# dt of every fourth unit of a selective scan: spread by DMA from rows in DRAM instead of by TensorE

## The reference

```
x = x + layer(layernorm(x))            # layer: below
x = x + ffn(layernorm(x))              # silu(x W1) * (x W3), Hadamard, W2
# layer: h = u + mamba(rmsnorm(u));  h + (silu(g) * up) @ down.T   (704 wide)
# mamba: z, x, B, C, dt_raw = split(rmsnorm(u) @ in_proj.T)
dt = softplus(dt_raw @ dt_proj.T + bias)          # 256 channels
for t in range(1024):                              # per channel, 32 states
    h = exp(dt[t] * A) * h + dt[t] * x[t] * B[t]
    y[t] = sum over states of h * C[t]
```

## Time and profile before

| | before |
|---|---|
| median of 3 runs | 1200.27 us |
| profiled execution | 1197.15 us |
| its span, first to last instruction | 1195.4 us |
| PE / PEld busy | 1069.9 / 539.2 us |
| DVE busy | 1021.0 us |
| POOL busy | 925.3 us |
| ACT busy | 603.6 us |
| scans run from | 51.2 to about 1091 us |
| moved by DMA | 176.38 MB |

### The profile page before, as it was taken

One profiled execution on the slowest core, in us unless ns is written; L12 is line 12 of the kernel. 1 busy time (PEld: TensorE's weight loads), 2 busy tenths in 40 slices (PEclk: granted clock), 3 DMA queues, 4 the chain that ended last, 5 costly groups with the idle time before them and its releaser, 6 DMA issues.

```text
span 1195.4 us, 12998 instructions
## 1 busy us (share of the span) xinstructions
PE 1069.9 (90%) x3848; PEld 539.2 (45%) x3848; DVE 1021.0 (85%) x1161; ACT 603.6 (50%) x1092; POOL 925.3 (77%) x564
## 2 busy tenths in 40 slices
PE   2577679999999999999998999899998989997988
PEld 1222124545544464446444554546453554445535
DVE  3379889999999989999999999999999999995322
ACT  3645366555654455555754555646654554443120
POOL 0479999878998889887998899878998898774000
PEclk9676559999999999999999999999999999899989
DMA  5898877765767676776768676867667576540000
GB/s 216 192 251 190 191 170 159 163 154 128 193 154 164 136 174 156 171 162 142 182 140 177 139 180 138 185 137 173 168 144 163 122 178 151 130 89 18 1 1 18
DMA packets 99493, 176.38 MB, mean 148 GB/s; under 512 B 12960, under 2 KB 21600, under 8 KB 98784
## 3 DMA queue, kind: packets, MB, share of 16 engines
q1 hardware_dynamic: 98272, 171.36, 62.9%
q0 software_dynamic: 1152, 4.19, 1.0%
HBM read 150.34 MB, written 8.39 MB: 133 GB/s over the span
## 4 chain that ended last, share of the span: by engine, by line
PE 56%; POOL 13%; DVE 10%; issue 10%; ACT 5%; DMA 3%; SPq 1%; DVEq 0%; POOLq 0%; ACTq 0%
PE p_r L444 17%; PE p_r L433 13%; POOL h_s L939 8%; PE p_r L439 8%; PE p_dt L388 7%; PE p_y L399 6%; DVE h_s L752 5%; PE p_r L450 3%; POOL bt_s L919 3%; DVE bt_s L737 2%; DMA bt_s<-dx_rows 2%; ACT p_dt L526 2%; ACT tok L543 1%; PE p_r L423 1%; ACT tok L541 1%
## 5 line engine op out<-in xcount | busy, mean ns | idle before, releaser
L939 POOL TENSOR_TENSOR h_s<-h_s,c_s 128x1024 f32<-128x1024 f32 x256 | 604.2, 2361 | 86.8 <-DVE h_s L752 76.6
L526 ACT ACTIVATE p_dt<-p_dt,an_s 128x512 f32<-128x512 f32 x512 | 331.3, 658 | 327.5 <-PE p_dt L388 327.1
L388 PE MATMUL p_dt<-kdt,pick_s 128*128 128x512 f32 x512 | 327.8, 665 | 47.3 <-DVE h_s L752 46.9
L752 DVE TENSOR_TENSOR_SCAN h_s<-p_dt,carry,bt_s 128x512 f32<-128x512 f32 x256 | 321.2, 1272 | 8.2 <-ACT p_dt L526 5.8
L752 DVE TENSOR_TENSOR_SCAN h_s<-p_dt,bt_s 128x512 f32<-128x512 f32 x256 | 305.1, 1212 | 26.0 <-ACT p_dt L526 15.8
L444 PE MATMUL p_r<-nT,w_s 128*128 128x512 f32 x512 | 243.9, 605 | 3.2 <-ACT nT L677 3.1
L919 POOL TENSOR_TENSOR bt_s<-bt_s,b_s 128x1024 f32<-128x1024 f32 x96 | 227.1, 2366 | 13.8 <-DMA bt_s<-dx_rows 13.7
L737 DVE TENSOR_TENSOR bt_s<-bt_s,p_b 128x1024 f32<-128x1024 f32 x160 | 192.5, 1203 | 5.1 <-DMA bt_s<-dx_rows 5.1
L388 PEld LDWEIGHTS p_dt<-kdt,pick_s 128*128 128x128 f32 x512 | 100.4, 202 | 204.5 <-DVE h_s L752 128.7
L433 PE MATMUL p_r<-nT,gu_s 128*128 128x512 f32 x352 | 169.4, 605 | 2.7 <-ACT nT L672 2.7
L399 PE MATMUL p_y<-h_s,ysel_s 128*32 128x512 f32 x1024 | 148.0, 652 | 16.6 <-POOL h_s L939 16.6
(11 more groups left out here) (86 smaller groups left out, 734.5 us busy)
## 6 DMA issues: line engine op xcount, KB each, us to landing
bt_s<-dx_rows SPq DMA_DIRECT2D x512, 256.0 KB, 5.3
kdt<-st_dt SPq DMA_DIRECT2D x64, 128.0 KB, 5.3
tok<-in_x SPq DMA_DIRECT2D x8, 512.0 KB, 7.1
xr_s<-xb_s SPq DMA_DIRECT2D x64, 64.0 KB, 3.9
dx_rows<-dx_s SPq DMA_DIRECT2D x16, 256.0 KB, 5.1
b_s<-xb_s SPq DMA_DIRECT2D x64, 64.0 KB, 4.9
xo<-in_x SPq DMA_DIRECT2D x8, 512.0 KB, 7.1
out<-res POOLq DMA_DIRECT2D x8, 512.0 KB, 5.5
```

The source lines that it names most:

```text
L388: nc.tensor.matmul(p_dt[DT_BANK[u]][:, :], sel, kdt[:, h, p // 16, :], start=True, stop=True)\
L526: A(p_dt[DT_BANK[u]][:, :], p_dt[DT_BANK[u]][:, :], ACT.Exp, scale=an_s[:, c:c + 1]).then_inc(a_dA, 1)
L752: V.tensor_tensor_scan(h_s[:, u % 8, :], p_dt[DT_BANK[u]][:, :], bt_s[:, u % 16, :], carry[:, u:u + 1] if par else 0.0, ALU.mult, ALU.add) ...
L939: G.tensor_tensor(h_s[:, two, :], h_s[:, two, :], c_s[:, h, :].unsqueeze(1).broadcast_to([P, 2, T]), ALU.mult)\
```

## The change

From the second tile on (i >= 1), units 3, 7, 11, ..., 63 (`ROW_UNITS`, 16 of 64) get no `spread`. Instead `keep_rows` also writes `dt_s` to DRAM (`dt_rows`), and `load_row_pair` reads the rows of two such units, each row repeated over 32 partitions, into a new tile `dtr4_s` of four places. `decay` of such a unit reads `dtr4_s` and still writes the PSUM bank `p_dt`, once the scan that used the bank last is done. Nothing else is reordered.

```
+ROW_UNITS = range(3, U, 4)
+def by_row(i, u):
+    return i >= 1 and u in ROW_UNITS
+def spreads(i, u):
+    return u + 1 if i == 0 else U + (i - 1) * (U - len(ROW_UNITS)) + u + 1 - made(ROW_UNITS, u)
...
+            def load_row_pair(t, par, q):
+                sp.wait_ge(l_dt_rows, ((t - 1) * 2 + q // 4 + 1) * 16)
+                sp.wait_ge(a_dA, t * U + 8 * q - 8)
+                for g in range(GH):
+                    rows_of_g = dt_rows[par, q // 4].rearrange("(a b g) t -> g a b t", a=4, g=GH)[g, 3]
+                    src = rows_of_g[2 * (q % 4):2 * (q % 4) + 2]
+                    sp.dma_start(dtr4_s[NS * g:NS * g + NS, 2 * (q % 2):2 * (q % 2) + 2, :],
+                                 src.partition_broadcast(NS)).then_inc(l_row4[q % 2], 16)
             def keep_rows(t, par, h):
+                if t >= 1:
+                    sp.wait_ge(a_dt, t * 2 + h + 1)
+                    sp.dma_start(dt_rows[par, h], dt_s[:, :]).then_inc(l_dt_rows, 16)
...
                 for u in range(U):
+                    if u % 8 == 2:
+                        q = u // 8 + 1
+                        if (units and i >= 1 if q < 8 else units and pre):
+                            load_row_pair(i + q // 8, par if q < 8 else 1 - par, q % 8)
...
-                    if (units if u + 2 < U else pre):
+                    if not by_row(i + (u + 2) // U, (u + 2) % U) and (units if u + 2 < U else pre):
                         spread(i + (u + 2) // U, (u + 2) % U)
...
-                act.wait_ge(pe_dt, i * U + u + 1)
                 c = UH * (u // UH) + unit_channel(u)
-                A(p_dt[DT_BANK[u]][:, :], p_dt[DT_BANK[u]][:, :], ACT.Exp, scale=an_s[:, c:c + 1]).then_inc(a_dA, 1)
+                if by_row(i, u):
+                    q = u // 8
+                    act.wait_ge(l_row4[q % 2], ((i - 1) * 4 + q // 2 + 1) * 64)
+                    act.wait_ge(v_sc, i * U + u - DT_GAP[u] + 1)
+                    dt_in = dtr4_s[:, u // 4 % 4, :]
+                else:
+                    act.wait_ge(pe_dt, spreads(i, u))
+                    dt_in = p_dt[DT_BANK[u]][:, :]
+                A(p_dt[DT_BANK[u]][:, :], dt_in, ACT.Exp, scale=an_s[:, c:c + 1]).then_inc(a_dA, 1)
...
                         act.wait_ge(g_dx, m)
+                        if m > 2:
+                            act.wait_ge(l_dt_rows, (m - 2) * 16)
                     A(dt_s[:, :], v, ACT.Copy).then_inc(a_dt, 1)
```

More of the change, by code:

```diff
@@ L128, in build @@
         bt_s = sb("bt_s", [P, RUN * 4, T])
+        dtr4_s = sb("dtr4_s", [P, 4, T])
         h_s = sb("h_s", [P, 8, T])
@@ L163, in build @@
         l_x, l_xo, l_xrep, l_out = sem("l_x"), sem("l_xo"), sem("l_xrep"), sem("l_out")
-        l_rows = sem("l_rows")
+        l_rows, l_dt_rows = sem("l_rows"), sem("l_dt_rows")
+        l_row4 = [sem(f"l_row4{k}") for k in range(2)]
         l_dx = [sem(f"l_dx{k}") for k in range(4)]
@@ L193, in build @@
         dx_rows = nc.dram_tensor("dx_rows", [2, 2, P, T], F32).ap()
+        dt_rows = nc.dram_tensor("dt_rows", [2, 2, P, T], F32).ap()
         x_t = x.rearrange("b s d -> (b s) d")
@@ L268, in load_dt @@
             def load_dt(t, h):
-                made_dt, spread_dt = number(t * 2 + h + 1), number((t - 1) * U + UH * (h + 1))
+                made_dt, spread_dt = number(t * 2 + h + 1), spreads(t - 1, UH * (h + 1) - 1) if t else 0
                 sp.wait_ge(a_dth, made_dt)
```

## The result

The changed kernel takes 1191.97 us (median of 4 runs, 1191.76 to 1193.68) against 1200.3 us for the kernel before beside it (1199.26 to 1201.45): ratio 0.9934, 95% interval 0.9916 to 0.9951. It gained 8.3 us; 17.3 were forecast. The direction held, and so did the outer range (1169 to 1200 us); the forecast band of 1176 to 1190 us was missed by 2 us, and the size is less than half of the forecast.

A forecast was written before the change was run, and what follows sets the result against it. TensorE and VectorE were both nearly full in tiles 1 to 7, with TensorE leading the last chain. 1197.15 - 19.3 + 1.6 = 1179.5 us, 1182.6 as a median, stated as 1183; band 1176 to 1190, outer range 1169 to 1200 us.

The forecast's parts named there:

- A spread's price: On TensorE: each spread costs 0.23 us, so 112 removed spreads take 25.8 us off it.
- Part B: Gate/up/down phase: five spreads fall away, 1.15 us per tile, 8.0 us over 7 tiles; bounds 0 and 12.6 us.
- Part A: End of the tile: w2's last group no longer cut by unit 63's spread; 0.55 us in six tiles, 3.3 us.
- the seam's 1.15: End of the tile: the second half of w2's last group starts 1.15 us earlier once both halves are one piece.
- Part C: w1/w3 phase: five spreads go and the wait behind the second softplus comes earlier; 1.15 us per tile, 8.0 us.
- The sum: Whole kernel: 3.3 + 8.0 + 8.0 = 19.3 us gained from the removed spreads.
- rival 2: Tiles 1 to 7: VectorE is the bound and the rest is hidden; 0 to 2 us gained, 1199 us; chance 0.12.
- The clock: Gap behind the down projection: TensorE's clock fell in one tile of seven; one more fall forecast, costing 1.6 us.
- rival 1: Gaps behind the down projection: the clock falls in every one, six more falls cost 9.8 us; 1190.8 us; chance 0.14.
- The DMAs at nothing: Added row reads and writes: DMA share rises from 0.67 to 0.83 in tiles 1 to 7, costing no time.
- The five other units at nothing: Spreads of units 3, 7, 11, 35 and 59 lie where TensorE waits for others; removing them gains nothing.
- The markers: Signs to check in the profile, such as TensorE busy time down over 25 us, tile period about 129 us.

The follow-up runs named there:

- e5: Changed kernel with only unit 63 by row, against the kernel before: 1196.83 us, ratio 0.9971.
- e6: Changed kernel with only units 15, 19, 23, 27 and 31 by row, against the kernel before: 1196.86 us, ratio 0.9971.
- e7: Changed kernel with only units 39, 43, 47, 51 and 55 by row, against the kernel before: 1196.73 us, ratio 0.9979.
- e1: Changed kernel without the added DMAs, exps of the units by row reading a constant 0.01: 1193.25 us, ratio 0.9943 to the kernel before.
- e2: Kernel before with the added DMAs issued and waited for but unused, all spreads kept on TensorE: 1200.99 us, ratio 1.0005.
- e17: e9 with 11 units by row; 3, 7, 11, 35 and 59 are spread by TensorE again: 1186.8 us, ratio 0.9883 to the kernel before.
- e9: Changed kernel plus two repeated matmuls ahead of c0's first step in six gaps, nothing moved: 1186.44 us, ratio 0.9883 to the kernel before.
- e10: Kernel before plus two repeated matmuls ahead of c0's first step in six gaps, nothing moved: 1196.68 us, ratio 0.9971.

## Why the prediction came out as it did

**A spread's price** held. With both engines relieved the five spreads of part B shorten their stretch by 1.08 us, where 5 x 0.23 = 1.15 was forecast.

**Part A** was right, in mechanism and nearly in size: 0.55 forecast, 0.74 measured (the ledger), 3.5 us alone (e5). That GpSimd's queue holds back more is shown: relieved, it lets 1.46 through, and in after the pass behind its norm waits 1.99 us where it waited 0.78. But 1.46 is more than the seam's 1.15, and with both engines relieved it is 0.74 again. Whether units 3, 7 and 11 gave the surplus, and what holds the stretch in the last pair, no run here tells.

**Part B** is the step that failed first: "VectorE had 42 - 40.2 = 1.8 us idle in it, so the room is there." 0.47 of 1.15 us arrived, 7 x 0.47 = 3.3 us (e6 alone: 3.5) and not 8.0. Idle time isn't room where it is spread over small waits of a chain through several engines: L880 still waits 1.20 us (1.05 before) at the end of a stretch that is shorter. With GpSimd relieved 0.59 arrives, with VectorE 0.83, with both 1.08: VectorE held most of what was missing, and GpSimd a part.

**Part C** failed too, by a step that could have been checked: "it comes earlier with that queue". 0.38 of 1.15 us arrived, 2.7 us (e7 alone: 2.5). The prediction has the second softplus wait for its matmul in TensorE's queue. It doesn't, not even before: in the odd tile of the earlier trace rows ScalarE goes from an exp through table load and softplus without idle time.

```profile
678.28 0.66 ACT L526 ACTIVATE p_dt<-p_dt,an_s 128x512 f32<-128x512 f32 x1
678.96 1.28 ACT L555 ACT_TABLE_LOAD   x1
680.25 0.66 ACT L555 ACTIVATE p_r<-p_r,par_s 128x512 f32<-128x512 f32 x1
```

So the wait behind it hardly moved: in the even tile 0.54 us in the earlier trace rows and 0.57 now, in the odd one 1.18 and 0.90. ScalarE's timeline in after:

```profile
543.98 0.69 ACT L564 ACTIVATE p_dt<-dtr_s,an_s 128x512 f32<-128x512 f32 x1
544.68 1.28 ACT L593 ACT_TABLE_LOAD   x1
545.98 0.66 ACT L593 ACTIVATE p_r<-p_r,par_s 128x512 f32<-128x512 f32 x1
546.66 1.28 ACT L564 ACT_TABLE_LOAD   x1
547.96 0.66 ACT L564 ACTIVATE p_dt<-p_dt,an_s 128x512 f32<-128x512 f32 x1
```

From one exp to the next, over two table loads and a softplus, it is 547.96 - 543.98 = 3.98 us, and the p_dt banks let ScalarE be no more than three units ahead. Nothing of those 3.98 us is TensorE's. That most of C's rest is held by VectorE is shown: 0.91 arrives with VectorE relieved, 0.36 with GpSimd.

**The sum.** By experiment alone A, B and C give 3.5 + 3.5 + 2.5 = 9.5 us, by the ledger 0.74 x 6 + 0.47 x 7 + 0.38 x 7 = 10.4, and by medians with the clock kept up 10.2. 19.3 was forecast. So rival 2 (the rest is hidden) held for about two thirds of B and C, with VectorE as the main holder but not the only one, and not for A.

**The clock** was mis-sized, from a false count. "In one tile of seven" rested on two gaps; there were three in that trace. After has six: three more where one was forecast, and what spoke against rival 1 ("six gaps of the same length kept 1.00") wasn't so. By the distances a fall costs 1.1 us in the mean and not 1.6, so three more cost some 3 us; in medians the added loss is 2.0 us, not clear of noise. That the forecast's 1.6 us lies near is luck: too few falls, each priced too high. It is luck too that rival 1's 1190.8 us stand next to the measured 1191.97: its mechanism was at work at a fifth to a third of its price of 9.8 us, and the shortfall of parts B and C made up the rest.

**The DMAs at nothing** was right: the share rose to 0.85 in tiles 1 to 7 (forecast 0.83), with a landing of 5.5 us, no wait after tile 0, and e1 and e2 on either side. **The five other units at nothing** was right as far as e17 can tell.

**The markers.** TensorE's busy time fell by 23.2 us and not "more than 25", w2's wait fell to 3.0 us in three times, L840's wait was "unchanged", which I had named as the sign of being wrong, ScalarE's waits for the spread fell from 327.1 to 270.6 us, by 17% and not a quarter, and the period fell from about 131.9 to 131.4 us in after with its falls, 130.1 without (e9); about 129 was forecast.

**Open.** With both engines relieved the gain is 17.9 us and 112 x 0.23 = 25.8 us were taken off TensorE; part of that lies beside waits (the five other units, and what part A left). What still holds C (0.90) and the last stretch (0.74) below 1.15 with both relieved wasn't tried. Nor is it settled why a given gap keeps its clock and the next doesn't.

## What to carry to other kernels

An engine's gain is worth what the next engine lets through, and idle time summed over a stretch isn't that: ask for each wait what it hangs on (here table loads, GpSimd's norm). Here a third to two fifths of parts B and C arrived, beside a VectorE that is 95% busy and a GpSimd that is 87% busy in tiles 1 to 7. Part experiments tell it cheaply, and relieving one engine at a time, with and without the change, tells who holds the rest. And taking work from TensorE can cost its clock: count every gap of every tile at the low level before and after, in more than one execution, and try two repeated matmuls in the gap, which here were worth 5.5 us in the changed kernel, where no one part of the change is worth more than 3.5.

## What the runs showed of the hardware

- The granted clock falls to 1.2 GHz in a gap where TensorE is sparsely busy between two dense stretches, in some tiles and not in others with the same program (three of seven before, six of seven after, one execution each). In the gap of after shown above TensorE's longest idle time was 1.86 us. Two repeated matmuls (0.86 us of TensorE's time each) kept the clock at 1.00 in all six gaps that had them, in e9 and in e10; the seventh gap had none and fell in both.
- A fall costs about 1.1 us from the down projection to w1 (8.6 to 8.7 us without one, 9.3 to 10.0 and 9.7 in the mean with one; the seventh gap, without next tile's work, left out).
- Exp from SBUF into PSUM took 685 ns, from PSUM into PSUM 659 ns (128x512): 26 ns more, inside the prediction's bounds of 0.1 us.
- Between exp and softplus ScalarE's table load took 1.28 us, and the ACTIVATE started 0.02 us behind it.
- Raising the DMA share in tiles 1 to 7 from 0.67 to 0.85 moved the landing of a 256 KB read only from 5.3 to 5.5 us.
